# A fused attention and expert kernel: ScalarE writes the rounded rows; router logits as four full-precision products, each in a column quadrant

## The chip, the cores and the metric

The kernel runs on one core of a Trainium2 chip. The metric is the device time of one execution in microseconds (us); lower is better. Before the change it is 1982.76 us, the median of three runs (1981.57 to 1986.39).

## What is computed

The reference is one transformer layer on 8192 rows of width 512 (4 batches of 2048): a modulated layer norm, attention within segments of 128 rows plus an attention among the first rows of the segments, a second modulated layer norm, and a mixture of 16 experts that sends each row to the expert with the largest router logit, up to 512 rows each. Cut to what matters:

```
h = _layernorm(x) * (1 + ca) + sa
x = x + ga * attention(h, Wq, bq, Wk, bk, Wv, bv, Wo, bo)     # local (128 x 128) + global part
h = _layernorm(x) * (1 + cb) + sb
score = softmax(h @ Wg + bg)                                  # 8192 x 16
gate, idx = max(score), argmax(score)
pos = rank of the row within its expert;  keep = pos < 512
y = relu(buf @ W1 + b1) @ W2 + b2                             # per expert, 512 -> 2048 -> 512
x = x + gb * where(keep, y[idx, pos] * gate, 0)
```

The choice of expert hangs on the logits, so they are computed with more precision than one pass of rounded operands gives.

## The kernel before

It is written by hand for the five engines, each with its own queue in program order; semaphores alone tie them together. Three stages follow one another: a prologue (products of weights, the modulation rows, the global attention), the attention over 16 groups of 512 rows (4 segments each), and the 16 experts.

Nearly all large products are made in three matmuls of rounded operands: an operand A is kept as A_hi (rounded to fp32r) and A_lo (the rest, A - A_hi), and `split3` (L320) issues hi*hi, hi*lo and lo*hi. So each operand that is computed on the chip needs two writes, a rounding and a subtraction.

The attention stage is a software pipeline. `iteration(i, ...)` stands once in each engine's block and works on group i, and on later steps of the groups i-1 (p1), i-2 (p2) and i-3 (p3). For TensorE (L690) the order is:

1. `g_tile` 0 and 1 of group i: the product of M with the rows h of group i, 12 matmuls each; tile 0 waits for `ht_split` chunk by chunk (L609).
2. The 16 transposes of h2 of group i-2 into four PSUM banks (L706), which wait for `h2_ready` from GpSimd; then `ranks` of group i-3.
3. `g_tile` 2; the transposes of the probabilities of group i-1 (L717); `g_tile` 3.
4. The product of probabilities and values of group i-1 (L733, L734), then the values U of group i (L744, 48 matmuls).
5. The router logits of group i-2: four matmuls with 32 stationary columns (Wg_hi and Wg_lo side by side) over h2t_hi, then four with 16 columns over h2t_lo, all accumulated in the same PSUM rows (L751, L753).
6. The 16 transposes of the normalised rows of group i+1 (L602), chunk k behind `u_split` k; the transposes of the logits (L765); the scores of group i (L774), full-precision fp32.

The steps that the change touches are these. ScalarE's `modulate` (L952) turns each transposed chunk into `ht`, 128x512. VectorE's `split_rows` (L1215) then makes `ht_hi` by a copy (L1219) and `ht_lo` by a subtraction (L1221), and it is the last step of VectorE's iteration (L1412). ScalarE writes `h2t_hi` (L1032), VectorE `h2t_lo` (L1368). ScalarE's `empty_parts` (L1009) moves the logits from PSUM to `logit_parts`; TensorE transposes them into `pt_bank`; VectorE's `route_logits` (L1285) adds the bias to the first half and then the second half, and goes on to the argmax. In VectorE's queue an iteration runs: maximum of the scores (L1350), `route_logits`, probabilities (L1363), `h2t_lo`, statistics of group i+1 (L1150), `pt_lo` (L1374), `route_slots`, the attention result `h` and `xr` (L1387, L1391), statistics of group i-1, two `u_lo`, `query_const` (L1275), two `u_lo`, `split_rows`. GpSimd normalises the rows of group i+1 (L1578), and scales and shifts h2 of group i-1 in eight instructions (L1621, L1625).

Of the kernel before, what the change touches and what calls it, by code (L numbers as in the profile page):

```python
# [60 lines left out]
def build_block(nc, x, wq, bq, wk, bk, wv, bv, wo, bo, wg, bg, w1, b1, w2, b2, cond, wmod, out):  # L61
# [63 lines left out]
    grows = [keep(f"grows{i}", [P, D], BF16) for i in range(2)]  # L125
    wg_s = keep("wg_s", [P, KC, E], F32)
    wg_split = keep("wg_split", [P, KC, 2 * E], F32R)
    b1_col = keep("b1_col", [P, E * H // P], F32)
# [46 lines left out]
    h2 = over(r_h2, ("h2_0", full, F32), ("h2_1", full, F32))  # L175
    h2t_hi, = over(r_h2t, ("h2t_hi", full, F32R))
    h2t_lo, = over(cursor[0], ("h2t_lo", full, F32R))
    seg_sq = [P, GS, P]
    prob, pt_hi, pt_lo = over(r_p, ("prob", seg_sq, F32), ("pt_hi", seg_sq, F32R), ("pt_lo", seg_sq, F32R))
    logit_parts, = over(r_p + 4 * KB, ("logit_parts", [2 * E, ROWS], F32))  # L180
    batch_rows = [P, NBATCH, D]
# [59 lines left out]
    def sem(name):  # L241
        return stack.enter_context(nc.semaphore(name))
# [3 lines left out]
    ident_made = sem("ident_made")  # L246
    init_made = sem("init_made")
    cond_in, bias_in, wv_in, wo_in, summ_in = (sem(f"{k}_in") for k in ("cond", "bias", "wv", "wo", "summ"))
    wqk_in = [sem(f"wqk_in{k}") for k in range(KC)]
    wm_in = [sem(f"wm_in{i}") for i in range(6)]  # L250
    wg_ready = sem("wg_ready")
    wg_in, bg_in, bo_in, bqk_in, b1_in = (sem(f"{k}_in") for k in ("wg", "bg", "bo", "bqk", "b1"))
# [15 lines left out]
    ln1_step, ln1_ready, ln1_rstd, xn_done = (sem(k) for k in ("ln1_step", "ln1_ready", "ln1_rstd", "xn_done"))  # L268
    t1_full, ht_full, ht_hi_done, ht_split, qc_raw, qc_ready = (sem(k) for k in (
        "t1_full", "ht_full", "ht_hi_done", "ht_split", "qc_raw", "qc_ready"))  # L270
    gt_full, gt_done, u_full, u_hi_done, u_split = (sem(k) for k in (
# [9 lines left out]
    h2_stored = [sem(f"h2_stored{i}") for i in range(2)]  # L281
    h2t_full, h2t_hi_done, h2t_split, parts_full, parts_out, lg_full = (sem(k) for k in (
        "h2t_full", "h2t_hi_done", "h2t_split", "parts_full", "parts_out", "lg_full"))
    lg_step, route, route_exp, pos_full = (sem(k) for k in ("lg_step", "route", "route_exp", "pos_full"))
    scattered = [sem(f"scattered{i}") for i in range(2)]
# [23 lines left out]
    def stand_alone(eng, passed):  # L309


        eng.sem_inc(passed, 1)
# [39 lines left out]
    def _(sp):  # L352
# [24 lines left out]
        for i, b in enumerate((bq, bk)):  # L377
# [7 lines left out]
            .then_inc(b1_in, 16)  # L385
        sp.dma_start(wg_s[:], wg.rearrange("(c p) e -> p c e", p=P)).then_inc(wg_in, 16)
        sp.wait_ge(init_made, 2)
# [131 lines left out]
    def _(pe):  # L519
# [152 lines left out]
        pe.wait_ge(v_split, KC)  # L672
        pe.wait_ge(wg_ready, 2)
        pe.wait_ge(made, POOL_MADE)
# [15 lines left out]
        def iteration(i, cur, prev, prev2, nxt, prev3):  # L690
# [19 lines left out]
            if g_tiles:  # L710
                if prev2:
                    pe.wait_ge(h2t_split, 4 * p2.n + 1)
                g_tile(i, 2)
# [5 lines left out]
            if g_tiles:  # L719
                if prev2:  # L720
                    pe.wait_ge(h2t_split, 4 * p2.n + 2)
                g_tile(i, 3)
            if prev:

                pe.wait_ge(u_split, 4 * p1.n + 4)
                pe.wait_ge(pt_split, p1.n + 1)
                pe.wait_ge(grows_in[p1.par], 16 * (p1.half + 1))
                if prev2:
                    pe.wait_ge(h2t_split, 4 * p2.n + 4)
                for s in range(GS):  # L730
                    if cur:
                        pe.wait_ge(gt_done, 4 * n + s + 1)
                    split3(pe, big[s][:, :], pt_hi[:, s, :], pt_lo[:, s, :], u_hi[:, s, :], u_lo[:, s, :], True, False)  # L733
                    pe.matmul(big[s][:, :], seg_sel[:, s, :], grows[p1.par][:], start=False, stop=True) \  # L734
                        .then_inc(av_full, 1)
            if cur:
                for s in range(GS):
# [7 lines left out]
                    last.then_inc(u_full, 1)  # L745
            if prev2:


                pe.wait_ge(h2t_split, 4 * p2.n + 4)
# [170 lines left out]
    def _(act):  # L920
# [78 lines left out]
        def iteration(i, cur, prev, prev2, nxt, prev3):  # L999
# [126 lines left out]
    def _(dve):  # L1126

        dve.memset(table_init[:, :, 0:1], NO_TOKEN).then_inc(init_made, 1)
        dve.memset(table_init[:, :, 1:2], 0).then_inc(init_made, 1)
# [68 lines left out]
        def floor_gate(row):  # L1198
# [8 lines left out]

        dve.wait_ge(wg_in, 16)
        dve.tensor_copy(wg_split[:, :, 0:E], wg_s[:]).then_inc(wg_ready, 1)
        dve.wait_ge(wg_ready, 1)  # L1210
        dve.tensor_tensor(wg_split[:, :, E:2 * E], wg_s[:], wg_split[:, :, 0:E].bitcast(F32), ALU.subtract) \
            .then_inc(wg_ready, 1)
# [72 lines left out]
        def route_logits(g):  # L1285

            r = RT * g.n
            dve.wait_ge(lg_full, g.n + 1)
            parts = pt_bank[:, 0:GS * 2 * E].rearrange("p (s c) -> p s c", c=2 * E)
# [54 lines left out]
        def iteration(i, cur, prev, prev2, nxt, prev3):  # L1344
# [14 lines left out]
            if prev:  # L1359
# [361 lines left out]
```

## Time and profile before

| | before |
|---|---|
| median of three runs | 1982.76 us (1981.57 to 1986.39) |
| the profiled execution | 1988.57 us, its span 1986.8 us |
| mean granted TensorE clock | 0.972 of 2.4 GHz |
| TensorE matmul busy | 1866.8 us (94%) |
| VectorE busy | 1315.1 us (66%) |
| ScalarE busy | 780.6 us (39%) |
| GpSimd busy | 863.5 us (43%) |

The busy shares are means over the three stages. The prologue ends near 110 us of the span, the attention stage near 722 us, and after a passage the experts run from about 795 us to the end. Instructions are named by engine, line, output and inputs. A full-precision fp32 matmul appears as two records, one for each pass of weights.

### The profile page before, as it was taken

How to read it: one execution, taken by the hardware profiler on the slowest of the kernel's cores; microseconds unless marked ns; L12 is line 12 of the kernel's file. 1: busy time of each engine (PE TensorE's matmuls, PEld its weight loads, DVE VectorE, ACT ScalarE, POOL GpSimd, SP SyncE). 2: the span in 40 equal slices, each digit the busy share in tenths (PEclk: the TensorE clock that was granted, in tenths of full speed). 3: DMA queues.
4: the chain of work that ended last, by engine and by line, in shares of the span. 5: the costliest groups of instructions: out<-in, count | busy, mean ns of one | idle time of the engine just before them, and what ended most of it. 6: DMA issues, size and time to landing. Idle time of an engine off the chain costs nothing.

```text
span 1986.8 us, 28205 instructions
## 1 busy us (share of the span) xinstructions
PE 1866.8 (94%) x9137; PEld 1517.2 (76%) x9138; DVE 1315.1 (66%) x2006; ACT 780.6 (39%) x1257; POOL 863.5 (43%) x709
## 2 busy tenths in 40 slices
PE   8998999989998973999999999999899999999998
PEld 3476777767777752788888888888888888888886
DVE  4378899998999875445655555354756878454763
ACT  2333333333343421333443433334535655333541
POOL 2034455644555443134434334233655766342632
PEclk9999999999999985999999999999999999999999
DMA  7143222332224342344354434434554556434531
GB/s 259 32 144 134 86 86 85 124 130 85 85 86 154 100 149 68 103 170 151 121 182 141 163 133 135 161 116 162 190 174 143 202 178 220 139 131 166 190 110 64
DMA packets 137916, 270.77 MB, mean 136 GB/s; under 512 B 17634, under 2 KB 18222, under 8 KB 137863
## 3 DMA queue, kind: packets, MB, share of 16 engines
q1 hardware_dynamic: 115338, 221.27, 31.8%
q0 software_dynamic: 22528, 48.86, 7.5%
q8 instruction: 29, 0.48, 0.1%
q14 instruction: 21, 0.16, 0.0%
HBM read 237.71 MB, written 50.72 MB: 145 GB/s over the span
## 4 chain that ended last, share of the span: by engine, by line
PE 70%; DVE 20%; issue 6%; ACT 2%; POOL 1%; DMA 1%; DVEq 0%; POOLq 0%; ACTq 0%; SPq 0%
PE bank L322 21%; PE bank L323 21%; PE bank L324 21%; DVE stats L1150 3%; DVE ht_hi L1219 3%; DVE ht_lo L1221 2%; DVE prob L1275 2%; DVE h L1387 2%; DVE xr L1391 2%; DVE u_lo L1409 1%; DVE h2t_lo L1368 1%; PE bank L817 1%; PE bank L563 1%; PE bank L531 1%; PE bank L591 1%
## 5 line engine op out<-in xcount | busy, mean ns | idle before, releaser
L1448 DVE TENSOR_TENSOR h_lo<-h_f,h_hi 128x512 fp32r<-128x512 f32 x256 | 221.0, 884 | 368.2 <-ACT h_f L1088 368.1
L1087 ACT ACTIVATE h_hi<-bank,b_col 128x512 fp32r<-128x512 f32 x256 | 176.4, 689 | 601.7 <-PE bank L324 589.9
L322 PE MATMUL bank<-bt_hi,w_hi 128*128 128x512 f32 (+4 forms) x1024 | 361.4, 353 | 7.8 <-DVE w_lo L1419 5.6
L323 PE MATMUL bank<-bt_lo,w_hi 128*128 128x512 f32 (+4 forms) x1024 | 360.3, 352 | 0.0
L324 PE MATMUL bank<-bt_hi,w_lo 128*128 128x512 f32 (+4 forms) x1024 | 360.2, 352 | 0.0
L322 PE MATMUL bank<-w_hi,h_hi 128*128 128x512 f32 x832 | 327.3, 393 | 3.8 <-DVE h_lo L1448 2.6
L323 PE MATMUL bank<-w_lo,h_hi 128*128 128x512 f32 x832 | 325.4, 391 | 0.0
L324 PE MATMUL bank<-w_hi,h_lo 128*128 128x512 f32 x832 | 325.1, 391 | 0.0
L322 PEld LDWEIGHTS bank<-bt_hi,w_hi 128*128 128x128 f32 x1024 | 195.4, 191 | 33.2 <-issue 9.0
L323 PEld LDWEIGHTS bank<-bt_lo,w_hi 128*128 128x128 f32 x1024 | 195.2, 191 | 21.1
L324 PEld LDWEIGHTS bank<-bt_hi,w_lo 128*128 128x128 f32 x1024 | 195.1, 191 | 20.4
L1644 POOL DMA_INDIRECT gb_rows<-mod_rows,tok_g x64 | 78.0, 1219 | 279.2 <-DVE tok_g L1525 221.7
L322 PEld LDWEIGHTS bank<-w_hi,h_hi 128*128 128x128 f32 x832 | 157.0, 189 | 36.9 <-issue 5.6
L324 PEld LDWEIGHTS bank<-w_hi,h_lo 128*128 128x128 f32 x832 | 156.9, 189 | 33.1
L323 PEld LDWEIGHTS bank<-w_lo,h_hi 128*128 128x128 f32 x832 | 157.1, 189 | 31.1
L1440 DVE TENSOR_TENSOR w_lo<-raw,w_hi 128x2048 fp32r<-128x2048 f32 x64 | 151.6, 2369 | 40.4 <-ACT w_hi L1077 40.4
L1644 POOL DMA_INDIRECT xh<-h_rows,tok_h x64 | 89.3, 1396 | 201.6 <-DVE tok_h L1507 178.2
L1088 ACT ACTIVATE h_f<-bank,b_col 128x512 f32<-128x512 f32 x256 | 174.3, 681 | 0.0
L1568 POOL TENSOR_TENSOR per_tok<-per_tok,half_neg 128x4 f32<-128x4 f32 (+1 forms) x33 | 33.4, 1013 | 279.7 <-DVE per_tok L1157 279.7
L1419 DVE TENSOR_TENSOR w_lo<-raw,w_hi 128x2048 fp32r<-128x2048 f32 x64 | 151.5, 2368 | 2.2
L322 PE MATMUL bank<-ht_hi,m_hi 128*128 128x512 f32 x256 | 113.6, 444 | 33.6 <-DVE ht_lo L1221 31.0
L1670 POOL TENSOR_TENSOR yo<-yo,gb_rows 128x512 f32<-128x512 f32 x60 | 98.5, 1642 | 106.4 <-DVE yo L1469 105.0
(256 smaller groups left out, 3375.1 us busy)
## 6 DMA issues: line engine op xcount, KB each, us to landing
raw<-in_L_ffn_W_dram SPq DMA_DIRECT2D x128, 1024.0 KB, 5.5
xa<-in_L_attn_x_dram SPq DMA_DIRECT2D x16, 1024.0 KB, 5.4
xr<-in_L_attn_x_dram SPq DMA_DIRECT2D x16, 1024.0 KB, 8.0
out_dram<-xr SPq DMA_DIRECT2D x16, 1024.0 KB, 9.9
h_rows<-h SPq DMA_DIRECT2D x16, 1024.0 KB, 4.6
b_bc<-in_L_ffn_b_dram SPq DMA_DIRECT2D x16, 256.0 KB, 6.3
wm_b<-in_L_wmod_dram SPq DMA_DIRECT2D x2, 1024.0 KB, 8.3
wm_d<-in_L_wmod_dram SPq DMA_DIRECT2D x2, 1024.0 KB, 5.1
```

The lines of the kernel that those rows point to most:

```text
L322: pe.matmul(o, a_hi, b_hi, start=start, stop=False)
L323: pe.matmul(o, a_hi, b_lo, start=False, stop=False)
L324: return pe.matmul(o, a_lo, b_hi, start=False, stop=stop)
L1087: act.activation(h1_hi[b % 2][:, j, :], h_bank[j][:, :], ACT.Relu, bias=bias)
L1088: act.activation(h1_f[:, j, :], h_bank[j][:, :], ACT.Relu, bias=bias).then_inc(relu_done, 1)
L1150: dve.bn_stats(st[0:parts, s, :], rows[:, s, :]).then_inc(step, 1)
L1219: dve.tensor_copy(ht_hi[:, k, :], ht[g.par][:, k, :]).then_inc(ht_hi_done, 1)
L1419: dve.tensor_tensor(w1_lo[b % 2][:], raw[2 * (b % 2)][:], w1_hi[b % 2][:].bitcast(F32), ALU.subtract) \
L1440: dve.tensor_tensor(w2_lo[b % 2][:], raw[2 * (b % 2) + 1][:], w2_hi[b % 2][:].bitcast(F32), ALU.subtract) \
L1448: dve.tensor_tensor(h1_lo[b % 2][:, j, :], h1_f[:, j, :], h1_hi[b % 2][:, j, :].bitcast(F32), ALU.subtract) \
L1644: pool.indirect_dma_start(out=rows[:, j, :], out_offset=None, in_=source, in_offset=bass.IndirectOffsetOnAxis(tokens[:, j:j + 1], 0), boun ...
L1670: pool.tensor_tensor(yo[:, j, :], yo[:, j, :], gb_rows[:, j, :], ALU.mult).then_inc(y_scaled, 1)
```

## The change

Rows of h: ScalarE's `modulate` reads each transposed chunk twice and writes both the rounded `ht_hi` and the full `ht`. VectorE's copy into `ht_hi` goes away; the subtraction stays.

Router logits: h2 transposed is kept once, in fp32 (`h2t`), and not split. Wg is kept once too, padded with zeros from 16 to 32 columns per quarter of the width. Each of the four quarters becomes one full-precision matmul of its own, whose output lies in PSUM rows 0-31, 32-63, 64-95 or 96-127, so that the four use different 32-column strips of the array, and none accumulates. ScalarE copies all 128 rows out; TensorE transposes four blocks of 128x128 in place of 32x128; VectorE sums the four quarters with a reduction and then adds the bias. TensorE's waits on `h2t_split` become waits on `h2t_done` from ScalarE, and the transposes get one more wait, that VectorE has read the previous group's (`lg_step`). The splitting of Wg in the prologue goes, and a memset of `wg_s` comes ahead of its load.

```diff
@@ TensorE
             if prev2:
-                pe.wait_ge(h2t_split, 4 * p2.n + 4)
+                pe.wait_ge(h2t_done, 4 * p2.n + 4)
                 for k in range(KC):
-                    pe.matmul(lg_bank[0:2 * E, :], wg_split[:, k, :], h2t_hi[:, k, :], start=(k == 0), stop=False)
-                for k in range(KC):
-                    last = pe.matmul(lg_bank[0:E, :], wg_split[:, k, 0:E], h2t_lo[:, k, :],
-                                     start=False, stop=(k == KC - 1))
+                    last = pe.matmul(lg_bank[k * QUAD:(k + 1) * QUAD, :], wg_s[:, k, :], h2t[:, k, :],
+                                     start=True, stop=True)
                 last.then_inc(parts_full, 1)
...
                 stand_alone(pe, pe_passed)
+                wait_past(pe, lg_step, p2.n)
                 for s in range(GS):
-                    last = pe.transpose(pt_bank[:, s * 2 * E:(s + 1) * 2 * E], logit_parts[:, chunk(s)],
-                                        ident[0:2 * E, 0:2 * E])
+                    last = pe.transpose(pt_bank[:, chunk(s)], logit_parts[:, chunk(s)], ident[:])
@@ ScalarE, modulate
-                act.activation(ht[g.par][:, k, :], big[k][:, :], ACT.Identity,
-                               bias=mod_col[:, 0, k, bass.ds(batch_of(g), 1)],
-                               scale=mod_col[:, 1, k, bass.ds(batch_of(g), 1)]).then_inc(ht_full, 1)
+                for rows in (ht_hi, ht[g.par]):
+                    ins = act.activation(rows[:, k, :], big[k][:, :], ACT.Identity,
+                                         bias=mod_col[:, 0, k, bass.ds(batch_of(g), 1)],
+                                         scale=mod_col[:, 1, k, bass.ds(batch_of(g), 1)])
+                ins.then_inc(ht_full, 1)
@@ ScalarE
-                act.activation(logit_parts[:], lg_bank[0:2 * E, :], ACT.Copy).then_inc(parts_out, 1)
+                act.activation(logit_parts[:], lg_bank[:, :], ACT.Copy).then_inc(parts_out, 1)
-                    act.activation(h2t_hi[:, k, :], big[(k + 2) % 4][:, :], ACT.Copy).then_inc(h2t_hi_done, 1)
+                    act.activation(h2t[:, k, :], big[(k + 2) % 4][:, :], ACT.Copy).then_inc(h2t_done, 1)
@@ VectorE, split_rows
                 dve.wait_ge(ht_full, 4 * g.n + k + 1)
-                dve.tensor_copy(ht_hi[:, k, :], ht[g.par][:, k, :]).then_inc(ht_hi_done, 1)
-                dve.wait_ge(ht_hi_done, 4 * g.n + k + 1)
                 dve.tensor_tensor(ht_lo[:, k, :], ht[g.par][:, k, :], ht_hi[:, k, :].bitcast(F32), ALU.subtract) \
@@ VectorE, route_logits
-            dve.tensor_tensor(lg[:], parts[:, :, 0:E], bg_bc[:].unsqueeze(1).to_broadcast(tok4), ALU.add) \
-                .then_inc(lg_step, 1)
+            parts = pt_bank[:, :].rearrange("p (s k e) -> p s e k", k=KC, e=QUAD)
+            dve.tensor_reduce(lg[:], parts[:, :, 0:E, :], AX_X, ALU.add).then_inc(lg_step, 1)
             dve.wait_ge(lg_step, g.n + 1)
-            dve.tensor_tensor(lg[:], lg[:], parts[:, :, E:2 * E], ALU.add).then_inc(route, 1)
+            dve.tensor_tensor(lg[:], lg[:], bg_bc[:].unsqueeze(1).to_broadcast(tok4), ALU.add).then_inc(route, 1)
@@ VectorE, iteration
-            if prev2:
-                for k in range(KC):
-                    dve.wait_ge(h2t_hi_done, 4 * p2.n + k + 1)
-                    dve.tensor_tensor(h2t_lo[:, k, :], big[(k + 2) % 4][:, :], h2t_hi[:, k, :].bitcast(F32),
-                                      ALU.subtract).then_inc(h2t_split, 1)
```

## Rows read from the trace of the kernel before

**Rows 1.** Busy time by stretch: start:end, length, busy of each engine, granted clock.
```profile
core 0: us, PE busy (x) PEld busy (x) DVE busy (x) ACT busy (x) POOL busy (x), PEclk, DMA share, GB/s
194.91:686.95 492.04, 454.01 (x2364) 355.69 (x2364) 445.72 (x961) 183.85 (x372) 258.79 (x240) 0.98 0.29 101
721.67:795.00 73.33, 30.09 (x131) 22.38 (x132) 47.62 (x121) 14.96 (x32) 27.04 (x24) 0.63 0.39 132
795.00:1986.00 1191.00, 1168.06 (x5739) 1003.18 (x5737) 686.98 (x639) 508.12 (x698) 512.63 (x372) 0.99 0.44 152
```

**Rows 2.** Two single iterations of the attention stage, same columns.
```profile
441.50:481.30 39.80, 36.87 (x198) 28.97 (x197) 36.71 (x82) 15.43 (x31) 21.47 (x20) 1.00 0.30 105
481.30:523.50 42.20, 38.66 (x198) 30.11 (x197) 37.62 (x81) 15.27 (x31) 21.62 (x20) 0.96 0.29 102
```

**Rows 3.** Waits in 194.91 to 686.95: who waited for whom, us in total, times, longest.
```profile
PE bank L322 <- DVE ht_lo L1221: 25.0, 12, 2.1
DVE h2t_lo L1368 <- ACT h2t_hi L1032: 27.4, 12, 3.0
PE bank L602 <- DVE u_lo L1409: 9.0, 12, 1.0
```

**Rows 4.** Who waited for ht_lo in the whole span: us, times.
```profile
  PEld bank L322: 43.8, 29
  PE bank L322: 31.0, 15
```

**Rows 5.** TensorE in order of time, one iteration: start, length, instruction [idle before].
```profile
509.99 1.10 PE L751 MATMUL bank<-h2t_hi,wg_split 128*32 128x512 f32 x4
...
511.86 1.03 PE L602 MATMUL bank<-ident,xa 128*128 128x128 f32 x8
513.72 1.26 PE L602 MATMUL bank<-ident,xa 128*128 128x128 f32 x8 [0.83 <-DVE u_lo L1409]
514.91 0.43 PE L765 MATMUL bank<-ident,logit_parts 32*128 32x32 f32 x4
515.27 3.84 PE L774 MATMUL bank<-ht,gt 128*128 128x128 f32 x32
518.86 0.48 PE L322 MATMUL bank<-ht_hi,m_hi 128*128 128x512 f32 x1
...
523.65 0.50 PE L322 MATMUL bank<-ht_hi,m_hi 128*128 128x512 f32 x1
...
550.02 1.10 PE L751 MATMUL bank<-h2t_hi,wg_split 128*32 128x512 f32 x4
```

**Rows 6.** VectorE and GpSimd in the same iteration.
```profile
512.99 1.28 DVE L1409 TENSOR_TENSOR u_lo<-bank,u_hi 128x512 fp32r<-128x512 f32 x2
514.18 0.41 DVE L1219 CAST ht_hi<-ht 128x512 fp32r<-128x512 f32 x1
...
517.72 1.68 DVE L1221 TENSOR_TENSOR ht_lo<-ht,ht_hi 128x512 fp32r<-128x512 f32 x1
...
520.73 1.26 POOL L1625 TENSOR_TENSOR h<-h,sb_tab 128x512 f32<-128x512 f32 x1 [0.18 <-POOL h L1621]
...
522.90 0.69 DVE L1221 TENSOR_TENSOR ht_lo<-ht,ht_hi 128x512 fp32r<-128x512 f32 x1
...
534.18 0.68 DVE L1374 TENSOR_TENSOR pt_lo<-bank,pt_hi 128x512 fp32r<-128x512 f32 x1
```

**Rows 7.** ScalarE in the same iteration.
```profile
512.15 0.57 ACT L1011 ACTIVATE logit_parts<-bank 32x512 f32<-32x512 f32 x1
512.68 1.45 ACT L957 ACTIVATE ht<-bank,mod_col 128x512 f32<-128x512 f32 x2
```

**Rows 8.** Groups of TensorE at 20 to 40 us: shapes, count, busy us, mean ns.
```profile
L563 PE MATMUL bank<-wm_b,sc_t 128*4 128x512 f32 x8 | 3.6, 592 | 0.0
```

**Rows 9.** TensorE at the start of another iteration, at the low clock.
```profile
482.02 0.63 PE L323 MATMUL bank<-ht_lo,m_hi 128*128 128x512 f32 x1
482.45 0.63 PE L324 MATMUL bank<-ht_hi,m_lo 128*128 128x512 f32 x1
```

**Rows 10.** The last group's logits, after the attention stage.
```profile
754.73 0.69 DVE L1368 TENSOR_TENSOR h2t_lo<-bank,h2t_hi 128x512 fp32r<-128x512 f32 x1 [0.16 <-ACT h2t_hi L1032]
...
755.48 1.11 PE L751 MATMUL bank<-h2t_hi,wg_split 128*32 128x512 f32 x4 [1.23 <-DVE h2t_lo L1368]
```

More of the change, by code:

```diff
@@ L125, in build_block @@
     grows = [keep(f"grows{i}", [P, D], BF16) for i in range(2)]
-    wg_s = keep("wg_s", [P, KC, E], F32)
-    wg_split = keep("wg_split", [P, KC, 2 * E], F32R)
+    QUAD = P // KC
+    wg_s = keep("wg_s", [P, KC, QUAD], F32)
     b1_col = keep("b1_col", [P, E * H // P], F32)
@@ L175, in build_block @@
     h2 = over(r_h2, ("h2_0", full, F32), ("h2_1", full, F32))
-    h2t_hi, = over(r_h2t, ("h2t_hi", full, F32R))
-    h2t_lo, = over(cursor[0], ("h2t_lo", full, F32R))
+    h2t, = over(r_h2t, ("h2t", full, F32))
     seg_sq = [P, GS, P]
     prob, pt_hi, pt_lo = over(r_p, ("prob", seg_sq, F32), ("pt_hi", seg_sq, F32R), ("pt_lo", seg_sq, F32R))
-    logit_parts, = over(r_p + 4 * KB, ("logit_parts", [2 * E, ROWS], F32))
+    logit_parts, = over(cursor[0], ("logit_parts", [P, ROWS], F32))
     batch_rows = [P, NBATCH, D]
@@ L247, in build_block @@
     init_made = sem("init_made")
+    wg_cleared = sem("wg_cleared")
     cond_in, bias_in, wv_in, wo_in, summ_in = (sem(f"{k}_in") for k in ("cond", "bias", "wv", "wo", "summ"))
@@ L250, in build_block @@
     wm_in = [sem(f"wm_in{i}") for i in range(6)]
-    wg_ready = sem("wg_ready")
     wg_in, bg_in, bo_in, bqk_in, b1_in = (sem(f"{k}_in") for k in ("wg", "bg", "bo", "bqk", "b1"))
@@ L268, in build_block @@
     ln1_step, ln1_ready, ln1_rstd, xn_done = (sem(k) for k in ("ln1_step", "ln1_ready", "ln1_rstd", "xn_done"))
-    t1_full, ht_full, ht_hi_done, ht_split, qc_raw, qc_ready = (sem(k) for k in (
-        "t1_full", "ht_full", "ht_hi_done", "ht_split", "qc_raw", "qc_ready"))
+    t1_full, ht_full, ht_split, qc_raw, qc_ready = (sem(k) for k in (
+        "t1_full", "ht_full", "ht_split", "qc_raw", "qc_ready"))
     gt_full, gt_done, u_full, u_hi_done, u_split = (sem(k) for k in (
@@ L281, in build_block @@
     h2_stored = [sem(f"h2_stored{i}") for i in range(2)]
-    h2t_full, h2t_hi_done, h2t_split, parts_full, parts_out, lg_full = (sem(k) for k in (
-        "h2t_full", "h2t_hi_done", "h2t_split", "parts_full", "parts_out", "lg_full"))
-    lg_step, route, route_exp, pos_full = (sem(k) for k in ("lg_step", "route", "route_exp", "pos_full"))
+    h2t_full, h2t_done, parts_full, parts_out, lg_full = (sem(k) for k in (
+        "h2t_full", "h2t_done", "parts_full", "parts_out", "lg_full"))
+    lg_step = sem("lg_step")
+    route, route_exp, pos_full = (sem(k) for k in ("route", "route_exp", "pos_full"))
     scattered = [sem(f"scattered{i}") for i in range(2)]
@@ L385, in _ @@
             .then_inc(b1_in, 16)
-        sp.dma_start(wg_s[:], wg.rearrange("(c p) e -> p c e", p=P)).then_inc(wg_in, 16)
+        sp.wait_ge(wg_cleared, 1)
+        sp.dma_start(wg_s[:, :, 0:E], wg.rearrange("(c p) e -> p c e", p=P)).then_inc(wg_in, 16)
         sp.wait_ge(init_made, 2)
@@ L672, in _ @@
         pe.wait_ge(v_split, KC)
-        pe.wait_ge(wg_ready, 2)
+        pe.wait_ge(wg_in, 16)
         pe.wait_ge(made, POOL_MADE)
@@ L711, in iteration @@
                 if prev2:
-                    pe.wait_ge(h2t_split, 4 * p2.n + 1)
+                    pe.wait_ge(h2t_done, 4 * p2.n + 1)
                 g_tile(i, 2)
@@ L720, in iteration @@
                 if prev2:
-                    pe.wait_ge(h2t_split, 4 * p2.n + 2)
+                    pe.wait_ge(h2t_done, 4 * p2.n + 2)
                 g_tile(i, 3)
@@ L746, in iteration @@
             if prev2:
-                pe.wait_ge(h2t_split, 4 * p2.n + 4)
+                pe.wait_ge(h2t_done, 4 * p2.n + 4)
                 for k in range(KC):
-                    pe.matmul(lg_bank[0:2 * E, :], wg_split[:, k, :], h2t_hi[:, k, :], start=(k == 0), stop=False)
-                for k in range(KC):
-                    last = pe.matmul(lg_bank[0:E, :], wg_split[:, k, 0:E], h2t_lo[:, k, :],
-                                     start=False, stop=(k == KC - 1))
+                    last = pe.matmul(lg_bank[k * QUAD:(k + 1) * QUAD, :], wg_s[:, k, :], h2t[:, k, :],
+                                     start=True, stop=True)
                 last.then_inc(parts_full, 1)
@@ L1126, in _ @@
     def _(dve):
+        dve.memset(wg_s[:], 0.0).then_inc(wg_cleared, 1)
         dve.memset(table_init[:, :, 0:1], NO_TOKEN).then_inc(init_made, 1)
@@ L1205, in floor_gate @@
                                           op0=ALU.max, op1=ALU.mult))
[L1208 to L1212, printed above, removed]
         split_weights(VCH, [vo_f[:, c, :] for c in range(KC)], v_hi, v_lo, v_split, v_step)
@@ L1288, in route_logits @@
             dve.wait_ge(lg_full, g.n + 1)
-            parts = pt_bank[:, 0:GS * 2 * E].rearrange("p (s c) -> p s c", c=2 * E)
-            dve.tensor_tensor(lg[:], parts[:, :, 0:E], bg_bc[:].unsqueeze(1).to_broadcast(tok4), ALU.add) \
-                .then_inc(lg_step, 1)
+            parts = pt_bank[:, :].rearrange("p (s k e) -> p s e k", k=KC, e=QUAD)
+            dve.tensor_reduce(lg[:], parts[:, :, 0:E, :], AX_X, ALU.add).then_inc(lg_step, 1)
             dve.wait_ge(lg_step, g.n + 1)
-            dve.tensor_tensor(lg[:], lg[:], parts[:, :, E:2 * E], ALU.add).then_inc(route, 1)
+            dve.tensor_tensor(lg[:], lg[:], bg_bc[:].unsqueeze(1).to_broadcast(tok4), ALU.add).then_inc(route, 1)
             dve.wait_ge(route, r + 1)
```

## The prediction

> **What bounds the kernel now.** I read the busy times by stretch first. Of the span, 1191 us are the experts, where TensorE is busy 98% [rows 1]; the change touches no instruction there, so they stay. The attention stage holds twelve equal iterations in 492.04 us, 41.0 us each [rows 1]. In it neither TensorE (454.01 of 492.04) nor VectorE (445.72) is full: each waits for the other at some point of a loop. Single iterations come in two kinds, 39.8 us at clock 1.00 and 42.2 us at 0.96 [rows 2].
>
> The waits name the points. TensorE waits 25.0 us for `ht_lo`, in each of the twelve iterations, and 9.0 us for `u_lo`; VectorE waits 27.4 us for the h2t rows before it can make `h2t_lo` [rows 3]. Over the whole span the wait for `ht_lo` comes 15 times [rows 4], which belongs to 14 iterations (groups 2 to 15; the first has two).
>
> The timeline shows what the waits don't. Call the start of the logits Z = 509.99; the next Z is 550.02, 40.03 us later [rows 5]. The scores end, and tile 0 of g begins, at 518.86 = Z+8.87, but its last chunk begins at 523.65 = Z+13.66. Nine matmuls come before that chunk; 523.65 to 525.82 is what nine take at full speed, 2.2 us, so with its operands there it would begin at Z+11.1. VectorE is what it waits for: it finishes `u_lo` at 514.18 = Z+4.19 and then makes eight instructions in 9.3 us, the last from 522.90 [rows 6]. These eight are slow because GpSimd works beside them: the subtraction takes 1.68 us at 517.72 and 0.69 at 522.90, when GpSimd's last instruction (520.73, 1.26 us) is over [rows 6]. From the last chunk to the next Z are 26.37 us in which TensorE is nearly dense. So the loop is 13.66 + 26.37, and the first term is VectorE's.
>
> **Part 1, ScalarE rounds the rows.** Four copies leave VectorE's tail. What is left is four subtractions from Z+4.19. At the slow price (1.60 us from start to start, from the 1.68 us row) they end at Z+10.6; with the last at 0.69 us, at Z+9.7. Both are before the Z+11.1 at which TensorE can use the last chunk, so the wait of rows 3 goes, and TensorE itself sets the point.
>
> ScalarE pays for it: two instructions of `modulate` take 1.45 us, 0.68 from start to start [rows 7], so the four added ones cost 2.7 us. It begins at Z+2.7 now, at Z+3.0 if the logits take 2.2 us (part 2), and then has a chunk ready every 1.36 us: Z+4.4, 5.7, 7.1, 8.5. The subtractions could take them at Z+4.2, 5.8, 7.4, 9.0. So the first is 0.2 us late and the others are covered; the end moves from Z+10.6 to Z+10.8, and 0.3 us before Z+11.1 stay free. What ScalarE is late beyond that comes into the loop whole. Behind `modulate` in its queue come only the exponentials, which wait for VectorE's maximum.
>
> **Part 2, logits.** Before, eight matmuls from 509.99 to 511.86, 1.87 us [rows 5]. After, four full-precision ones. A full-precision matmul of 512 moving columns is two records of 0.44 us even with 4 stationary columns (3.6 us for eight records, four matmuls) [rows 8]. No row of the kernel before has two matmuls in different column strips, so their joint cost X is bounded: 3.5 us if they go one after another, 0.9 if all four stream together. I take 2.2: the two passes of one quarter share a strip and can't overlap, and in program order the second pass of one may run beside the first pass of the next, which makes five steps of 0.44. This lies nearer neither end; but it matters little. After the logits TensorE has two banks of transposes (0.93 us) and then waits until 513.72 = Z+3.73 for `u_lo` [rows 5], so any X up to 2.8 us is covered by that wait; beyond it each us costs a us, and at 3.5 the price is 0.7 us.
>
> The Trainium skill ("TensorEngine Tiling (Array Packing)", Key Properties) says that tiles in different strips run independently, which would put X at the low end, and also, against this change, that switching the tiling mode drains the array. The trace has 128-column and 32-column products back to back at Z, 0.23 us apart as inside a group, so no drain shows; by the first rule the sum below stays as it is.
>
> The four transposes of the logits cost 0.36 us now (514.91 to 515.27) [rows 5]. Blocks of 128 cost 0.117 each, as the sixteen of L602 do (0.93 us for eight), so 0.47: +0.11. Copying 128 rows in place of 32 takes ScalarE no longer per row of time (0.57 us for 512 columns [rows 7]; 0.60 at most, like its other copies of this length). The reduction reads 256 elements in place of 64: about 0.2 us more on VectorE, where it is hidden, since the probabilities are needed some 5 us later. The `lg_step` wait is met long before: the previous reduction is the first quarter of the same iteration. It holds up nothing.
>
> `h2t_lo` goes: four subtractions, 2.5 us, and the 2.3 us wait per iteration before them [rows 3]. I count no gain from it in the loop. Behind it stand the statistics and then `pt_lo`, which needs the transposes of TensorE anyway and starts at 534.18, as soon as ScalarE has rounded them [rows 6]. The gained time turns into a wait there. From `pt_lo` on VectorE runs without a stop to `u_lo`, and that leg keeps its 19 us. Left of the gain is slack for part 1: the statistics and the `modulate` of GpSimd come earlier.
>
> **The sum.** New iteration: 8.87 + 0.11 + 2.2 + 26.37 = 37.5 us against 41.0 (mean). The saving is 3.5 us; of it 2.5 are the wait itself, and 1.0 the share of iterations that fall to the low clock. There a matmul starts every 0.43 us and not 0.23 [rows 9]; such a fall follows the 2 us stop before the last chunk, which is gone. Fourteen iterations: 14 x 3.5 = 49 us. After the stage the last group's logits lie on the chain [rows 10]: `h2t_lo` 0.7 us less, matmuls 2.2 for 2.0, transposes and reduction +0.3: nothing. In the prologue ScalarE has 2.7 us more at 57 us of the span, where TensorE reaches the last chunk some 4 us later: nothing. The profiled execution would go from 1988.57 to 1939.6; the median of the runs lies 5.8 us lower, so 1982.8 - 49 = 1934 us.
>
> **Rivals.**
>
> Case A, as above: 1934, own range 1928 to 1940. Rows 3 and 6 speak for it: the wait is in every iteration, and the arithmetic leaves 0.3 us of slack.
>
> Case B, one strip after another: X = 3.5. The scores end at Z+9.4, `modulate` begins 0.8 us later on ScalarE as `empty_parts` waits for the last matmul, last chunk at Z+11.7. Iteration 38.1, saving 2.9 x 14 = 41, less 1.5 at the end: 1943. For it: in rows 5 matmuls of one strip follow each other at 0.23 us. Against: those share their strip and accumulate.
>
> Case C, the clock. With a small X TensorE idles up to 1.9 us behind the first two banks of transposes (0.83 now), and a fall of the clock could come there. A stretch at 0.43 us costs about 1.6 us; in every iteration that leaves 3.5 - 1.7 = 1.8 us, 25 in all: 1958. The mean clock would stay at 0.97.
>
> Case D, the leg from `pt_lo` shortens too. GpSimd's normalising would fall before `route_slots` and no longer beside it, and give back up to 1 us: 14 x 4.5 = 63: 1920.
>
> Case E, slower than before. Each product in a new strip makes the array run empty, at both passes. The iteration is X + 34.5, so the change loses from X = 6.5 us on, 1.6 us a matmul or 0.8 a pass. At X = 8 it is 42.5: +21 us, and +6 for the last two groups: 2010. Nothing in rows 5 speaks for it, where a change of width costs nothing.
>
> Case F, the change doesn't do what it says: `ht_lo` is late all the same, because `ht_full` comes after both writes and every subtraction is then held by GpSimd for more than one of its instructions. The same 9.3 us tail gives no gain: 1980.
>
> **Chances.** A 0.45, B 0.25, C 0.10, D 0.08, E 0.05, F 0.07. The predicted time is case A's. The range of 8 in 10 takes in A, B, D's and most of C: 1920 to 1957. About 0.3% (6 us) is what a measurement of this kernel can tell from no change. Faster by over 0.3%: A to D, 0.88. Within 0.3%: 0.06. Slower by over 0.3%: 0.06.
>
> **What would show it.** Right: no wait of TensorE for `ht_lo` in the attention stage (now 31.0 us in 15 times); iterations of 37 to 38 us; clock near 1.00 there; VectorE waiting 2 to 5 us per iteration for ScalarE's `pt_hi`; the copies of rows at 0.68 us from start to start. X is read from the first logits matmul to the next transposes: near 2 for A, 3.5 for B, over 6 for E. Wrong: the wait for `ht_lo` stays, or one for `h2_ready` takes its place, as GpSimd ends its eight instructions at Z+12 and TensorE now asks at Z+14; the experts' stretch differing from 1191 us by more than 2.

## The result, and the profile after

The changed kernel takes 1912.8 us (median, 1909.4 to 1915.5) against 1984.6 (1981.6 to 1989.2) for the kernel before on the same chip: ratio 0.9636, 95% interval 0.9609 to 0.9662. That is 72 us where 49 were forecast, and it lies below the range of 1920 to 1957. The profiled execution took 1909.39 us, its span is 1907.7.

Busy time by stretch after the change, with the columns of [rows 1]. The first line is the same twelve iterations, the second the passage, the third the experts:

```profile
core 0: us, PE busy (x) PEld busy (x) DVE busy (x) ACT busy (x) POOL busy (x), PEclk, DMA share, GB/s
183.89:615.72 431.83, 423.86 (x2364) 340.75 (x2364) 373.28 (x865) 215.06 (x420) 265.44 (x241) 1.00 0.34 116
648.30:721.60 73.30, 28.41 (x148) 21.24 (x149) 45.55 (x114) 16.61 (x35) 29.73 (x25) 0.72 0.40 133
721.60:1907.70 1186.10, 1162.91 (x5722) 998.25 (x5720) 686.47 (x638) 506.96 (x696) 509.76 (x371) 0.99 0.45 153
```

492.04 us have become 431.83: 35.99 us per iteration against 41.0, with TensorE busy 98% of them where it was 92%, and the granted clock at 1.00 where it was 0.98. The passage shows the same 73.3 us, but its window ends inside the experts, at no common event. From the last maximum of scores to the first product of the experts it is 66.3 us before and 64.2 after (64.0 in a second profile of the changed kernel), so about 2 us may have been gained there; in the other runs of this study that leave the rows whole it is 63.8 to 66.1 us. The experts differ by 5 us from [rows 1]. In those other runs the time from the last maximum of scores to the end is 1257.5 to 1262.2 us, in this profile 1259.4 and in the one of before 1265.2. As the kernel before was profiled once, this looks like spread between executions and not like the change, but that isn't shown. From the first scores to the last the profiles show 605.3 us before and 533.8 after, 71.5 less: as much as the whole change in the median.

The waits in the same twelve iterations answer [rows 3] (who waited for whom, us, times, longest):

```profile
DVE pt_lo L1361 <- ACT pt_hi L1036: 27.6, 12, 2.5
...
DVE ht_lo L1214 <- ACT ht L955: 13.1, 28, 1.4
PEld bank L603 <- DVE u_lo L1396: 11.6, 20, 1.3
...
PE bank L603 <- DVE u_lo L1396: 7.4, 10, 1.1
...
PE bank L322 <- DVE ht_lo L1214: 0.9, 2, 0.7
```

TensorE's 25.0 us for `ht_lo` have become 0.9, its 9.0 for `u_lo` 7.4. Over the whole span, where [rows 4] had 31.0 us in 15 waits, four are left:

```profile
  PEld bank L322: 4.9, 7
  PE bank L322: 2.0, 4
```

VectorE, which never waited at `pt_lo` before, now waits there for ScalarE's `pt_hi` 2.3 us in each iteration: its freed time comes to light at that point.

TensorE in order of time, one iteration, as [rows 5]. Z is 497.52 here:

```profile
497.52 1.06 PE L751 MATMUL bank<-h2t,wg_s 128*32 128x512 f32 x8
498.52 1.09 PE L603 MATMUL bank<-ident,xa 128*128 128x128 f32 x8
500.18 1.26 PE L603 MATMUL bank<-ident,xa 128*128 128x128 f32 x8 [0.57 <-DVE u_lo L1396]
501.27 0.60 PE L763 MATMUL bank<-ident,logit_parts 128*128 128x128 f32 x4
501.71 3.74 PE L771 MATMUL bank<-ht,gt 128*128 128x128 f32 x32
505.20 0.48 PE L322 MATMUL bank<-ht_hi,m_hi 128*128 128x512 f32 x1
...
507.37 0.39 PE L322 MATMUL bank<-ht_hi,m_hi 128*128 128x512 f32 x1
...
533.41 1.06 PE L751 MATMUL bank<-h2t,wg_s 128*32 128x512 f32 x8
```

The logits take 1.00 us from their start to the next transposes. The second transposes begin at Z+2.66 (in the next iteration at Z+3.17) where they began at Z+3.73, the scores end at Z+7.68 where they ended at Z+8.87, and tile 0 runs into its last chunk without a stop, at Z+9.85 where it was Z+13.66. Behind it come 26.0 us (26.37 before).

VectorE and ScalarE in that iteration, as [rows 6] and [rows 7]:

```profile
480.40 0.59 ACT L1036 ACTIVATE pt_hi<-bank 128x512 fp32r<-128x512 f32 x1
481.02 0.69 DVE L1361 TENSOR_TENSOR pt_lo<-bank,pt_hi 128x512 fp32r<-128x512 f32 x1 [2.53 <-ACT pt_hi L1036]
...
496.59 1.77 DVE L1268 SCALAR_TENSOR_TENSOR prob<-xa,vc_tab 128x512 f32<-128x512 f32 x1
...
499.45 1.28 DVE L1396 TENSOR_TENSOR u_lo<-bank,u_hi 128x512 fp32r<-128x512 f32 x2
...
500.88 0.69 DVE L1214 TENSOR_TENSOR ht_lo<-ht,ht_hi 128x512 fp32r<-128x512 f32 x1 [0.15 <-ACT ht L955]
502.22 1.03 DVE L1214 TENSOR_TENSOR ht_lo<-ht,ht_hi 128x512 fp32r<-128x512 f32 x1 [0.65 <-ACT ht L955]
503.56 3.06 DVE L1214 TENSOR_TENSOR ht_lo<-ht,ht_hi 128x512 fp32r<-128x512 f32 x2 [0.31 <-ACT ht L955]
```

The reader is to see three things. The four subtractions end at 506.54, Z+9.0, ahead of the last chunk; ScalarE's copies hold up three of them, by 0.15 to 0.65 us. `pt_lo` follows `pt_hi` at once. And `u_lo` begins at 499.45 = Z+1.93, where it began at Z+3.0.

### The profile page after: what moved, and what is told of

It reads as the page before. It is cut to its first block, busy times and chain, and to the rows that moved or that the text cites. A ratio compares the mean times of both kernels' runs of the same rounds, so it can differ in the third digit from the quotient of the medians.

```text
span 1907.7 us, 28124 instructions
## 1 busy us (share of the span) xinstructions
PE 1821.5 (95%) x9137; PEld 1490.8 (78%) x9138; DVE 1226.4 (64%) x1877; ACT 822.3 (43%) x1321; POOL 869.4 (46%) x709
## 4 chain that ended last, share of the span: by engine, by line
PE 80%; DVE 11%; issue 4%; ACT 2%; POOL 1%; DMA 1%; DVEq 0%; POOLq 0%; ACTq 0%; SPq 0%
PE bank L322 23%; PE bank L324 23%; PE bank L323 23%; PE bank L771 2%; PE bank L707 2%; DVE h L1374 1%; DVE prob L1268 1%; DVE stats L1150 1%; DVE xr L1378 1%; PE bank L814 1%; PE bank L564 1%; PE bank L603 1%; DVE ht_lo L1214 1%; PE bank L532 1%; DVE u_lo L1396 1%
## 5 line engine op out<-in xcount | busy, mean ns | idle before, releaser
L1076 ACT ACTIVATE w_hi<-raw 128x2048 fp32r<-128x2048 f32 x64 | 122.7, 1916 | 0.0
```

Source lines behind the costliest of these rows:

```text
L1076: act.activation(w2_hi[b % 2][:], raw[2 * (b % 2) + 1][:], ACT.Copy).then_inc(w2_hi_done, 1)
```

## The experiments

"Scores to scores" is the distance from one start of VectorE's maximum of scores to the next; its mean over groups 2 to 14 is the iteration, 41.00 us before and 35.99 after (35.93 in a second profile of the changed kernel). Ratios are against the kernel before on the same chip, 1985 us.

**Each part by itself.** `rows_alone` is the kernel before with part 1 only:

```diff
-                act.activation(ht[g.par][:, k, :], big[k][:, :], ACT.Identity, ...)
+                for rows in (ht_hi, ht[g.par]):
+                    ins = act.activation(rows[:, k, :], big[k][:, :], ACT.Identity, ...)
+                ins.then_inc(ht_full, 1)
...
-                dve.tensor_copy(ht_hi[:, k, :], ht[g.par][:, k, :]).then_inc(ht_hi_done, 1)
-                dve.wait_ge(ht_hi_done, 4 * g.n + k + 1)
```

> The kernel before with part 1 alone: ScalarE writes ht_hi and ht, VectorE only subtracts; the logits and h2t_lo stay as they were. Theory R (the wait for ht_lo was VectorE's tail): the tail falls from 9.3 us to 6.4, the iteration from 41.0 to about 37.4 us, the whole to 1984.6 - 14 x 3.6 = 1934 us, ratio 0.975. Theory S (the two parts only work together, because h2t_lo keeps VectorE full): VectorE's 37 us of work per iteration less 3.8 leaves it the bound, at about 39 us: 1956, ratio 0.986.

`logits_alone` is the rest of the change: the full-precision logits, and `h2t_lo` gone.

```diff
                 for k in range(KC):
-                    pe.matmul(lg_bank[0:2 * E, :], wg_split[:, k, :], h2t_hi[:, k, :], ...)
...
+                    last = pe.matmul(lg_bank[k * QUAD:(k + 1) * QUAD, :], wg_s[:, k, :], h2t[:, k, :],
+                                     start=True, stop=True)
...
-                    dve.tensor_tensor(h2t_lo[:, k, :], big[(k + 2) % 4][:, :], h2t_hi[:, k, :].bitcast(F32),
-                                      ALU.subtract).then_inc(h2t_split, 1)
```

> The change's part 2 alone: full-precision logits in four column strips, no h2t_lo; VectorE still copies ht_hi. Theory R as recorded before the result (h2t_lo is worth nothing in the loop): the tail of 9.3 us behind u_lo stays, iteration 41.0 us, whole 1984.6, ratio 1.00. Theory L (h2t_lo pushed pt_lo back by 0.6 us behind the statistics, and pushed GpSimd's normalising onto route_slots, so everything from pt_lo to u_lo came later): the iteration loses 1.0 to 1.5 us although the tail stays: about 39.8 us, whole 1968, ratio 0.991.

Measured: `rows_alone` 1929.7 us, ratio 0.9723 (0.9705 to 0.9741), iteration 37.05. `logits_alone` 1973.5 us, 0.9946 (0.9928 to 0.9965), iteration 40.09. Part 1 does what was forecast of it, a little better (37.05 for 37.4). Part 2 is worth 0.9 us per iteration, where 0 was expected, even while `ht_lo` still holds the loop. The two gains of the iteration add up: 3.95 + 0.91 = 4.86 of 5.01.

The waits of `logits_alone`, in the same twelve iterations:

```profile
DVE pt_lo L1361 <- ACT pt_hi L1034: 49.1, 12, 5.1
...
PE bank L322 <- DVE ht_lo L1214: 33.8, 22, 2.2
```

VectorE stands idle for 4.1 us at `pt_lo`, more than the 2.5 us of work that went, and still the iteration is shorter. So time is gained behind `pt_lo`, or `pt_lo` itself comes earlier in the loop, or TensorE had waited for `h2t_lo` itself.

**Only the four subtractions back.** `h2t_lo_back` is the changed kernel, with the four subtractions and TensorE's waits for them as before; nobody reads their result.

```diff
+            if prev2:
+                for k in range(KC):
+                    dve.wait_ge(h2t_done, 4 * p2.n + k + 1)
+                    wait_past(dve, h2t_split, 4 * p2.n + k - 2)
+                    dve.tensor_tensor(h2t_lo[:, k % 3, :], big[(k + 2) % 4][:, :], h2t[:, k, :],
+                                      ALU.subtract).then_inc(h2t_split, 1)
             if nxt:
                 stats1(i.plus(1))
```

> The changed kernel with the four subtractions of h2t_lo put back on VectorE at their old place, written to a place that nothing reads, and with TensorE's waits on them as before. Theory R: VectorE has 2.5 us idle before pt_lo, they fit in it, iteration stays at 36.0 us, ratio 0.964. Theory L: pt_lo is again 0.6 us or more late and GpSimd's normalising lies beside route_slots, iteration 37.0 to 37.5 us, 14 x 1.2 = 17 us more than the changed kernel: 1930, ratio 0.972.

Measured: 1927.0 us, 0.9714 (0.9693 to 0.9734); 36.97 us per iteration. (The expectations further down say 37.05 for this kernel; the mean of its twelve iterations is 36.97.) Theory L's figure is met and theory R's is not: `h2t_lo` costs 0.98 us per iteration. The three steps now part the whole gain: part 1 takes 1985.0 to 1929.7 (55.3 us), the other form of the logits 1929.7 to 1927.0 (2.8, within the spread of the runs of one kernel), the four subtractions 1927.0 to 1912.8 (14.1; the profiles have 12 to 13 less from the first scores to the last).

Rows of the kernel before, in the iteration of [rows 5], and of the same place in `h2t_lo_back`, show a first part of it:

```profile
532.98 0.59 ACT L1037 ACTIVATE pt_hi<-bank 128x512 fp32r<-128x512 f32 x1
...
530.99 2.46 DVE L1150 BATCH_NORM_STATS2 stats<-xa 128x6 f32<-128x512 f32 x4
533.61 0.38 DVE L1154 BATCH_NORM_AGGREGATE mv<-stats 128x2 f32<-128x6 f32 x4 [0.16 <-DVE stats L1150]
```

```profile
490.33 0.59 ACT L1037 ACTIVATE pt_hi<-bank 128x512 fp32r<-128x512 f32 x1
...
488.34 2.46 DVE L1151 BATCH_NORM_STATS2 stats<-xa 128x6 f32<-128x512 f32 x4
490.96 0.38 DVE L1155 BATCH_NORM_AGGREGATE mv<-stats 128x2 f32<-128x6 f32 x4 [0.16 <-DVE stats L1151]
...
491.52 0.68 DVE L1368 TENSOR_TENSOR pt_lo<-bank,pt_hi 128x512 fp32r<-128x512 f32 x1
```

Before, `pt_hi` is ready at 533.57, but `pt_lo` starts at 534.18 [rows 6]: VectorE is then still at the statistics, which stand behind the four subtractions. `h2t_lo_back` has the same 0.6 us (490.92 to 491.52). After the change `pt_hi` is ready at 480.99 and `pt_lo` starts at 481.02. No view of waits lists these 0.6 us, since VectorE doesn't wait in them: it works on something else.

Neither theory named the second part: TensorE itself waits for the first subtraction. `g_tile` 2 stands behind `h2t_split` in the kernel before and in `h2t_lo_back`, and behind ScalarE's `h2t_done` after the change. The last products of `ranks` and the first of `g_tile` 2, before, in `h2t_lo_back` and after:

```profile
528.99 0.22 PE L685 MATMUL bank<-onehot,ones 128*128 128x48 bf16 x3
529.34 0.50 PE L322 MATMUL bank<-ht_hi,m_hi 128*128 128x512 f32 x1
```

```profile
486.25 0.22 PE L687 MATMUL bank<-onehot,ones 128*128 128x48 bf16 x3
486.68 0.50 PE L323 MATMUL bank<-ht_hi,m_hi 128*128 128x512 f32 x1 [0.21 <-DVE h2t_lo L1362]
```

```profile
512.58 0.22 PE L686 MATMUL bank<-onehot,ones 128*128 128x48 bf16 x3
512.66 0.47 PE L322 MATMUL bank<-ht_hi,m_hi 128*128 128x512 f32 x1
```

The waits in the window of [rows 3] had it, in the row of the weight loads (PEld), 0.2 us in each of the twelve iterations; the second fence is `h2t_lo_back`:

```profile
PEld bank L322 <- DVE h2t_lo L1368: 2.7, 12, 0.2
```

```profile
PE bank L604 <- DVE u_lo L1403: 16.6, 12, 1.5
...
PE bank L323 <- DVE h2t_lo L1362: 1.7, 8, 0.2
```

The starts of TensorE's instructions, as means of twelve iterations, part the cost. From the last product of `ranks` to `g_tile` 2 it is 0.35 us in `h2t_lo_back` and 0.02 after the change, 0.33 less. From the first transposes to the second, where TensorE waits for `u_lo`, it is 2.35 and 1.63 us, 0.72 less. No other place differs by more than 0.04 us. So a third of the cost is TensorE's own stop before `g_tile` 2, and two thirds lie in its wait for `u_lo`.

**What else is in the 0.98 us?** In `h2t_lo_back` GpSimd's normalising (3.0 us) runs beside `route_slots`, which takes 3.28 us from 492.12; after the change it begins earlier and `route_slots` takes 2.93 us. Two kernels cut that normalising (L1565) to 8 of 512 columns, so that the rest of those rows stays unnormalised; one has the four subtractions and one has not.

```diff
-                pool.tensor_scalar(xa[g.par][:, s, :], xa[g.par][:, s, :], RS1[:, s:s + 1], ...
+                pool.tensor_scalar(xa[g.par][:, s, 0:8], xa[g.par][:, s, 0:8], RS1[:, s:s + 1], ...
```

> The version with the four subtractions h2t_lo put back (37.05 us per iteration) in which GpSimd's normalising of the rows for the next group covers 8 of 512 columns; the other columns stay unnormalised, so only the attention stage can be compared. Its VectorE work is untouched. Open is where the 1.06 us per iteration go that the four subtractions cost (37.05 against 35.99). Theory T (taking turns): part of it is GpSimd's normalising, which the later statistics move beside route_slots; then route_slots falls from 3.28 to 2.93 us and the iteration to about 36.7 us, the rest being the 0.6 us by which pt_lo starts late. Theory L (lateness alone): nothing but pt_lo's place in VectorE's queue matters; the iteration stays at 37.0 to 37.1 us.

> The changed kernel in which GpSimd's normalising of the rows for the next group covers 8 of 512 columns; the other columns stay unnormalised, so only the attention stage can be compared. With the same cut the version with the four subtractions h2t_lo back takes 36.21 us per iteration. Theory L (the 0.6 us by which pt_lo starts late is most of what h2t_lo costs): the distance of the two stays, and the iteration is 35.3 to 35.6 us. Theory T (the normalising beside route_slots is most of it): the cut makes the two alike, and the iteration is 36.0 to 36.2 us, as in the changed kernel as it is.

Measured: 36.21 us per iteration with the subtractions, 35.43 without (1916.0 and 1902.1 us in one execution each). The first is more than the taking of turns promised: 0.76 us go, not 0.35. The distance between the two is 0.78 us, where it is 0.98 without the cut. So that normalising is a small part at most of what `h2t_lo` costs. The lateness of `pt_lo` isn't thereby shown to be the rest: in this pair too TensorE stops before `g_tile` 2 (0.39 us from start to start against 0.03), which is 0.36 of the 0.78. The other 0.42 is a net figure, as in `norm_short_after` TensorE no longer waits for `u_lo` at all and other waits limit the loop. No run takes away TensorE's stop and leaves `pt_lo` late, or the other way about. The cut changes other meetings too. In the cut kernel without subtractions, for one, the last product of the values runs alone:

```profile
491.07 0.69 DVE L1268 SCALAR_TENSOR_TENSOR prob<-xa,vc_tab 128x512 f32<-128x512 f32 x1
```

In the changed kernel the same instruction meets GpSimd's first scaling of h2 and takes 1.77 us (496.59, shown above). That is ahead of `u_lo`, and makes it 1.1 us later. It isn't the whole of it either: the changed kernel has single iterations of 35.3 us and others of 36.1, and one of 35.36 has this instruction at 1.74 us. In the two iterations of 35.3 to 35.4 us from one Z to the next TensorE doesn't wait for `u_lo`. What frees them of that wait stays open.

**How four full-precision matmuls share the array.** `one_strip` and `two_strips` accumulate the four quarters in one strip of 32 columns, or in two (the diff is that of one; for two, `k % 2`, `k < 2` and `KC - 2`):

```diff
-                    last = pe.matmul(lg_bank[k * QUAD:(k + 1) * QUAD, :], wg_s[:, k, :], h2t[:, k, :],
-                                     start=True, stop=True)
+                    q = k % 1
+                    last = pe.matmul(lg_bank[q * QUAD:(q + 1) * QUAD, :], wg_s[:, k, :], h2t[:, k, :],
+                                     start=(k < 1), stop=(k >= KC - 1))
```

> The changed kernel, but the four full-precision matmuls of the logits accumulate in one 32-column strip (PSUM rows 0-31), in place of a strip each. Theory Q (strips stream together: 1.0 us for the four in the changed kernel's trace): here they take 3.5 us, of which 0.6 us hide behind the wait for u_lo, so the iteration goes from 36.0 to 37.9 us and the whole by 14 x 1.9 + 2 = 29 us, to 1941, ratio 0.978. Theory N (the matmuls are short for another reason, such as the few columns): they stay at 1.0 us and nothing changes, ratio 0.964.

> The changed kernel with the logits in two strips, quarters 0 and 2 accumulating in one and 1 and 3 in the other, issued 0, 1, 2, 3. A matmul of one strip takes 0.88 us alone. Theory Q (strips stream together in pairs): 4 matmuls take 1.8 to 2.0 us, covered by the wait for u_lo to within 0.3 us; iteration 36.0 to 36.3 us, whole about 1914. Theory H (a matmul overlaps only with a next one whose strip is not waited for, so accumulation makes them queue): 2.6 us or more, iteration 37 us.

TensorE's rows of `one_strip`, and then of `two_strips`:

```profile
518.01 3.62 PE L752 MATMUL bank<-h2t,wg_s 128*32 128x512 f32 x8
521.56 1.64 PE L603 MATMUL bank<-ident,xa 128*128 128x128 f32 x13
```

```profile
504.16 1.91 PE L752 MATMUL bank<-h2t,wg_s 128*32 128x512 f32 x8
506.00 2.13 PE L603 MATMUL bank<-ident,xa 128*128 128x128 f32 x16
```

The same eight passes take 3.55 us in one strip, 1.84 in two and 1.00 in four. So strips stream side by side, and the passes of one strip follow each other at 0.44 us. The Trainium skill ("TensorEngine Tiling (Array Packing)", Key Properties) says that tiles operate independently, and these three times agree. Its other rule there, that a change of mode drains the array, shows in no row as more than 0.1 us: in the changed kernel the transposes begin 1.00 us after the first logits product, which is two passes of 0.44 and 0.1 us, and the first logits product 0.32 us after the product of 128 columns before it, where [rows 5]'s kernel has 0.23. One strip costs the loop 1.9 us (37.89; 1939.9 us, 0.9774, 0.9756 to 0.9793), two 0.6 (36.63; 1918.9 us in one execution). The rest of the difference in X (2.55 and 0.84 us) falls to the wait for `u_lo`, 0.7 us of which is gone in both. With two strips half a microsecond comes back at the next wait: TensorE waits for `ht_lo` in each of the twelve iterations there, 4.7 us in all.

**GpSimd beside VectorE's tail.** `pool_short_before` is the kernel before with GpSimd's eight scalings and shifts of the h2 rows on 8 of 512 columns, the rest left as they are:

```diff
-                    pool.tensor_tensor(rows, rows, cb_tab[:, bass.ds(b, 1), :]..., ALU.mult) \
+                    pool.tensor_tensor(rows[:, 0:8], rows[:, 0:8], cb_tab[:, bass.ds(b, 1), 0:8]..., ALU.mult) \
```

> The kernel before, with GpSimd's eight scalings and shifts of h2 cut from 512 to 8 columns each; so h2 is left unscaled in the other 504, the rows go to other experts, and only the attention stage may be compared. Theory G (VectorE's tail is slow because its instructions take turns with GpSimd's): the four copies take 0.41 us each and the four subtractions 0.69, the tail 4.4 us in place of 9.3, no wait of TensorE for ht_lo, iteration about 36.8 us in place of 41.0. Theory V (the tail is VectorE's own work): the tail stays near 9 us, the iteration near 41.

Measured: 36.32 us per iteration, against 41.00, and no wait of TensorE for `ht_lo`. VectorE's tail there:

```profile
503.94 0.43 DVE L1219 CAST ht_hi<-ht 128x512 fp32r<-128x512 f32 x1 [1.21 <-ACT ht L957]
504.40 0.69 DVE L1221 TENSOR_TENSOR ht_lo<-ht,ht_hi 128x512 fp32r<-128x512 f32 x1
505.01 0.42 DVE L1219 CAST ht_hi<-ht 128x512 fp32r<-128x512 f32 x1
...
507.59 0.69 DVE L1221 TENSOR_TENSOR ht_lo<-ht,ht_hi 128x512 fp32r<-128x512 f32 x1
```

The same eight instructions take 4.3 us in place of the 9.3 of [rows 6]. The subtractions that took 1.68 us beside GpSimd take 0.69 alone. The Trainium skill ("SBUF — State Buffer", SBUF: two separate sides) has VectorE's instructions with two SBUF inputs and GpSimd's that read SBUF lock each other out of a shared pair of ports for a whole instruction. The trace agrees for the subtractions: with GpSimd's instructions at 0.2 to 0.5 us in place of 1.3 to 1.7, and over before the tail, they take 0.69 us. The copies, with one input, were slowed too, to 1.48 and 1.51 us (at 516.20 and 519.32 of the kernel before) from 0.42.

The same cut in the changed kernel asks what is left there:

> The changed kernel in which GpSimd's eight scalings and shifts of the h2 rows cover 8 of 512 columns; the other columns are left as they are, so only the attention stage can be compared. Theory G (GpSimd's turns on the four subtractions are all covered now, since TensorE no longer waits for ht_lo): the iteration stays at 35.3 to 36.0 us, u_lo and ScalarE's modulate being the limits. Theory H (VectorE's work beside GpSimd is still on the path in each iteration): it falls to TensorE's own work, 35.3 us (423.86 us in twelve iterations), in all iterations, and VectorE's wait for pt_hi grows from 2.3 us by what is saved.

```profile
core 0: us, PE busy (x) PEld busy (x) DVE busy (x) ACT busy (x) POOL busy (x), PEclk, DMA share, GB/s
181.27:600.39 419.12, 419.12 (x2354) 341.45 (x2365) 308.36 (x865) 214.22 (x420) 143.53 (x240) 1.00 0.36 124
```

34.93 us per iteration, and TensorE is busy in all of it: this is the floor of its own work. It is lower than the 35.3 that the expectation took from busy time, so busy time was not a floor. The changed kernel is 1.06 us above it, and this cut of GpSimd's work gives all of it back. So GpSimd's work was still on the path, as the second theory had it, and VectorE's wait for `pt_hi` grows to 3.45 us.

**Shortening the leg by order.** `slots_first` is the changed kernel with `route_slots`, which needs nothing new, ahead of `pt_lo`, in the 2.3 us in which VectorE waits. `after_again` is the changed kernel once more beside it.

```diff
+            if prev3:
+                route_slots(p3)
             if prev:
                 dve.wait_ge(pt_hi_done, p1.n + 1)
...
-            if prev3:
-                route_slots(p3)
```

> The changed kernel with VectorE's route_slots moved ahead of pt_lo, into the 2.3 us per iteration in which VectorE waits for pt_hi. Theory L (the leg from pt_lo to u_lo is what TensorE still waits for, 0.6 us per iteration): that wait goes, iteration 35.4 us, 14 x 0.6 = 8 us less than the changed kernel: 1905, ratio 0.960. Theory P (TensorE at 98% has no more to give, and pt_lo comes 0.7 us later, behind which the product of probabilities and values waits): 36.0 us or up to 0.3 more, ratio 0.964 to 0.966.

> The changed kernel once more, beside slots_first on the same chip: ratio 0.964 and 36.0 us per iteration, by every theory.

Measured: 1910.8 us, 0.9626 (0.9613 to 0.9640), against 1912.5, 0.9625 (0.9611 to 0.9639) for the changed kernel: no difference that can be told. The iteration is 35.71 and not 35.93 in one profile each. The waits of `slots_first`:

```profile
DVE ht_lo L1214 <- ACT ht L955: 28.2, 28, 1.8
PEld bank L322 <- DVE ht_lo L1214: 11.4, 16, 1.2
PE bank L322 <- DVE ht_lo L1214: 3.3, 6, 0.7
```

TensorE no longer waits for `u_lo`, but VectorE's wait for ScalarE's rows has doubled (13.1 us in the changed kernel): with `u_lo` early, the 5.4 us of `modulate` are the next thing that is late. No version that beats the changed kernel was found.

## Why the prediction was wrong

**The step that failed** is the one on `h2t_lo`: "I count no gain from it in the loop", because `pt_lo` "starts at 534.18, as soon as ScalarE has rounded them". It starts 0.6 us later than that. The row of `pt_hi` was not set beside it; its 0.59 us from 532.98 say 533.57, and the statistics fill the time between. And the prediction took `h2t_lo` for work that only `pt_lo` stands behind, but TensorE's `g_tile` 2 waits for its first chunk: the weight load before it waits 0.2 us for `h2t_lo` in every iteration. Measured by `h2t_lo_back`: 0.98 us per iteration, 14.1 us in all, two thirds of the 21 us by which the forecast missed. Of TensorE's idle time that went with the subtractions 0.33 us stood before `g_tile` 2 and 0.72 at `u_lo`. That the late `pt_lo` makes the 0.72 is argued from the rows and not shown by a run of its own. Rival D had named a gain on this leg, by GpSimd's normalising alone; its time of 1920 lay nearest, but the means it named is a small part at most.

**The leg keeps its 19 us**: this held nearly as said. From the start of `pt_lo` to that of the second `u_lo` it is 18.65 us before (534.18 to 552.83) and 18.43 after (481.02 to 499.45). But a leg that begins earlier in the loop ends earlier: against the next Z, `pt_lo` moved from Z-15.84 to Z-16.50.

**Part 1** was right in its mechanism, and a little too small. Waits for `ht_lo` gone, last chunk at Z+10.9 in `rows_alone` (forecast Z+11.1), 26.2 us behind it for 26.37, clock 1.00: 37.05 us where 37.4 were due without part 2's 0.11. The first interval saves 4.9 us (38.18 to 33.27, 33.29 in `rows_alone`) where 3.5 were counted, as two waits for `ht_lo` lay in that group; in the second profile of the changed kernel it is 34.50, so 3.7. Together 55 us for 49.

**The cost of four matmuls** X was taken at 2.2 us and measured 1.00. The sum hid it behind the wait for `u_lo`, so this moved little in the loop: the form of the logits is worth 2.8 us in all, which is within the spread of the runs. The bound of 3.5 is met by `one_strip` (3.55), and its price was put too low: 0.7 us of iteration for X of 3.5, measured 1.9. Cover that is a wait shrinks when the engine waited for gets faster: here `u_lo` had come 1.1 us earlier. That the passes of one quarter would make five steps of 0.44 was wrong; all four strips run together, two steps.

**The last interval** was left out of the sum, as it has no wait for `ht_lo`. It fell from 34.72 to 32.58 us. It is 34.40 in `rows_alone`, 33.66 with X of 1.00 in place of 1.87, 32.58 without the four subtractions. The second profile of the changed kernel has 33.20, so these steps hold to within 0.6 us.

**Right as forecast**: little in the passage (some 2 us, where nothing was counted), the reduction hidden, the transposes of the logits at 0.44 us for 0.36 (0.47 forecast), ScalarE's rows at 0.66 to 0.68 us from start to start (499.40, 500.08, 500.74), VectorE waiting 2.3 us for `pt_hi` (2 to 5 forecast), no wait for `h2_ready` among the rows of waits. ScalarE's slack of 0.3 us was what it looked like: VectorE now waits 13.1 us for its rows, which reaches TensorE in two of the twelve iterations, and is the limit in `slots_first`. Of the rivals, B (one strip after another), C (the clock falls), E and F did not occur. (The working of C prices a fall of the clock at 1.6 us and then takes off 1.7; nothing hangs on it.)

## What to carry to other kernels

Before a step on an engine is counted at nothing "because its successor waits for another engine anyway", set the end of that other engine's row beside the successor's start. If they differ, the engine was busy and not waiting, no list of waits shows it, and the difference can be a gain for every loop that runs through the successor. Then look for everyone else who waits for the step, short waits of the weight loads too: 0.2 us in each iteration stood in the list here. And what a removed wait used to cover must be priced anew, at the waits that are left after the change.

## What the runs showed of the hardware

- Full-precision matmuls with 32 stationary columns in four column strips ran together: eight passes of 0.44 us in 1.00 us, against 1.84 in two strips and 3.55 in one.
- VectorE's tail of eight instructions took 4.3 us alone and 9.3 us beside GpSimd's instructions of 1.3 to 1.7 us. GpSimd's work alone was worth 4.7 us of a 41.0 us iteration of the kernel before, and still 1.06 us of 35.99 after the change.
- With TensorE's stops of 2 us gone, the granted clock was 1.00 over the twelve iterations (2.4 GHz) where it had been 0.98.
